# Gated recurrence: the first rows of the second recurrence (keys and queries times gates) on GpSimd instead of VectorE

## The reference, cut to what matters

```python
def step(carry, inp):
    S, R = carry
    q_t, k_t, v_t, a_t, aR_t, b_t, g_t = inp
    kn = k_t / jnp.maximum(jnp.linalg.norm(k_t, axis=-1, keepdims=True), 1e-12)
    pred = jnp.einsum('bhji,bhj->bhi', S, kn)
    r = jnp.clip(v_t - pred, -CLIP, CLIP)
    S = a_t[..., None] * S
    kp = jnp.einsum('bhd,bhde->bhe', kn, S)
    S = S + b_t[..., None, None] * kn[..., None] * (v_t - kp)[..., None, :]
    o = jnp.einsum('bhji,bhj->bhi', S, q_t)
    R = aR_t[..., None] * R
    kpR = jnp.einsum('bhd,bhde->bhe', kn, R)
    R = R + g_t[..., None, None] * kn[..., None] * (r - kpR)[..., None, :]
    o = o + jnp.einsum('bhji,bhj->bhi', R, q_t)
    return ((S, R), o)
```

## Time and profile before

| what | value |
|---|---|
| median of 3 runs | 3036.23 us (3035.22 to 3039.76) |
| span of the profiled execution | 3029.5 us |
| the rounds of the recurrence, from the first `begin` to the last fill | 919.6 to 1910.3 us of the span |
| busy in that stretch (990.7 us) | PE 774.1, DVE 861.8, ACT 444.2, POOL 381.8 us |
| granted TensorE clock in that stretch | 0.92 of full speed |

### The profile page before, as it was taken

One profiled execution on the slowest core, in us unless ns is written; L12 is line 12 of the kernel. 1 busy time (PEld: TensorE's weight loads), 2 busy tenths in 40 slices (PEclk: granted clock), 3 DMA queues, 4 the chain that ended last, 5 costly groups with the idle time before them and its releaser, 6 DMA issues. The chain is left out here.

```text
span 3029.5 us, 119908 instructions
## 1 busy us (share of the span) xinstructions
PE 2443.0 (81%) x51995; PEld 1879.4 (62%) x51995; DVE 2046.8 (68%) x4945; ACT 1381.3 (46%) x3266; POOL 958.9 (32%) x1170
## 2 busy tenths in 40 slices
PE   8978477999976787877888787659998997798754
PEld 6755465555555576767767676547876554576633
DVE  3448336777748988989888889257777666664752
ACT  5443233444443445544444443437776554463420
POOL 0000324665640633344333344211111441261004
PEclk9979778999988899999999998879999998897876
DMA  3200431111110000000000000002222003242014
GB/s 100 63 1 29 122 105 53 46 46 46 46 62 3 4 4 4 5 4 4 4 4 4 4 4 4 3 17 60 63 60 67 3 3 106 59 110 68 6 42 120
DMA packets 80349, 118.09 MB, mean 39 GB/s; under 512 B 11360, under 2 KB 66160, under 8 KB 79296
## 3 DMA queue, kind: packets, MB, share of 16 engines
q1 hardware_dynamic: 71312, 100.66, 10.7%
q0 software_dynamic: 8576, 10.53, 1.7%
HBM read 98.51 MB, written 16.51 MB: 38 GB/s over the span
## 5 line engine op out<-in xcount | busy, mean ns | idle before, releaser
L3174 PE MATMUL psum<-l1d_rw,l1d_cols 64*32 64x32 f32 (+2 forms) x20480 | 244.4, 216 | 107.7 <-issue 88.1
L3174 PEld LDWEIGHTS psum<-l1d_rw,l1d_cols 64*32 64x32 f32 x20480 | 211.8, 108 | 151.2 <-issue 126.9
L2469 POOL TENSOR_SCALAR l1xs_p<-l1xs_p,l1xs_col 128x257 f32<-128x257 f32 x256 | 233.8, 932 | 204.7 <-DVE l1xs_col L2425 204.7
L2894 POOL TENSOR_TENSOR l1d_tmp<-l1d_lt,l1d_xi 128x64 f32<-128x64 f32 (+1 forms) x96 | 41.7, 463 | 634.0 <-DVE l1d_xi L3525 632.7
L2390 ACT ACTIVATE l1xs_p<-psum,l1xs_col 128x257 f32<-128x257 f32 x256 | 120.0, 474 | 209.1 <-DVE l1xs_col L2420 203.1
L3432 DVE TENSOR_TENSOR l1d_rw<-l1d_rw,l1d_tots 128x1536 f32<-128x1536 f32 x96 | 151.9, 1582 | 45.7 <-PE psum L3174 45.2
L2432 DVE STREAM_TRANSPOSE l1xs_pt<-l1xs_p 128x288 f32<-128x288 f32 x256 | 122.4, 478 | 79.4 <-POOL l1xs_p L2469 79.4
L3111 PE MATMUL psum<-l1d_src,l1d_wp 128*128 128x128 f32 x1024 | 139.0, 293 | 3.2 <-issue 1.9
L2354 PE MATMUL psum<-l1xs_pt,l1xs_vals 32*128 32x512 f32 x1152 | 136.6, 604 | 0.0
L2342 PE MATMUL psum<-l1xs_keys,l1xs_qx 128*32 128x257 f32 x2048 | 130.9, 389 | 4.3 <-DVE l1xs_qx L2414 2.8
L3111 PEld LDWEIGHTS psum<-l1d_src,l1d_wp 128*128 128x128 f32 x1024 | 128.4, 204 | 7.4 <-issue 4.1
(11 more groups left out here) (558 smaller groups left out, 6845.5 us busy)
## 6 DMA issues: line engine op xcount, KB each, us to landing
l2f_w<-in_l2f_w SPq DMA_DIRECT2D x16, 768.0 KB
l1xs_vals<-in_ctx_strips SPq DMA_DIRECT2D x16, 576.0 KB
l0f_w<-in_l0f_w SPq DMA_DIRECT2D x15, 579.0 KB
l0x_ctxT<-in_ctxT SPq DMA_DIRECT2D x16, 516.0 KB, 3.7
l1xs_keys<-in_ctxT SPq DMA_DIRECT2D x16, 516.0 KB
l2x_ctxK<-in_ctxT SPq DMA_DIRECT2D x64, 129.0 KB, 2.1
l2x_ctxV<-in_ctxT SPq DMA_DIRECT2D x64, 129.0 KB, 2.1
l3f_w<-in_l3f_w SPq DMA_DIRECT2D x15, 193.5 KB
```

The lines of the kernel that those rows point to most:

```text
L2469: nc.gpsimd.tensor_scalar(p[:, t % 4, :S2], p[:, t % 4, :S2], col[:, 2, t % 4:t % 4 + 1], None, ALU.mult).then_inc(s["norm"], 1)
L3174: mm = nc.tensor.matmul(k.ps[bank0 + pr + e // per * 2][b * T:b * T + T, e % per * w:(e % per + 1) * w], cols[rr, 2 * n, e * 128 + b * T:e ...
```

## The change

`begin` for R leaves DVE. A new function `begin_r` on POOL does the same three multiplications. POOL runs it for round 0 ahead of its loop, and for round i + 1 ahead of the merges of round i. DVE gets a wait on `rowR` in level 0 of `advance`, since that step overwrites the keys' products that POOL read.

```diff
+            def begin_r(i):
+                odd = lambda x: x.rearrange("p g (n two) -> p g n two", two=2)[:, :, :, 1]
+                even = lambda x: x.rearrange("p g (n two) -> p g n two", two=2)[:, :, :, 0]
+                pool.wait_ge(s["kn"], i * 8 + 8)
+                pool.wait_ge(s["q"], i * 2 + 2)
+                pool.wait_ge(s["gate"], i * 4 + 4)
+                if i > 0:
+                    pool.wait_ge(s["mR_mm"], i * LEVELS)
+                tt(rw[:, 6], rw[:, 1], ar[:], ALU.mult)
+                tt(even(rw[:, 5]), odd(rw[:, 3]), even(ar[:]), ALU.mult)
+                tt(odd(rw[:, 5]), odd(rw[:, 4]), odd(ar[:]), ALU.mult).then_inc(s["rowR"], 1)
+
+            begin_r(0)
             for i in range(NT):
+                if i + 1 < NT:
+                    begin_r(i + 1)
                 pool.wait_ge(s["turn"], 2 * i + 2)
...
                 dve.wait_ge(s[mm], i * LEVELS + lv + 1)
+                if lv == 0:
+                    dve.wait_ge(s["rowR"], i * LEVELS + 1)
...
             begin(0, a, 0, 2, "rowS")
-            begin(0, ar, 6, 5, "rowR")
...
                     begin(i + 1, a, 0, 2, "rowS")
-                    begin(i + 1, ar, 6, 5, "rowR")
```

## The result

| | before | changed |
|---|---|---|
| median, us | 3035.72 (3034.02 to 3039.76, 4 runs) | 3100.09 (3097.84 to 3106.03, 4 runs) |
| ratio to before | | 1.0214, 95% interval 1.0197 to 1.0232 |
| span of the profiled execution, us | 3029.5 | 3104.2 |

The change costs 64 us, 2.1%. The forecast was 3084 (48 us), its range 3058 to 3106. The profiled execution of the changed kernel took 3106.03 us with a span of 3104.2, so 1.8 us lie around the span, not the 6.7 I assumed; the traced execution of the kernel before was some 4 us faster than its median, and the two spans lie 74.7 us apart.

The account below looks back on a forecast made before the run. No engine was full; the S rows and the fill before `keep_s` set the pace. Span 3029.5 plus 16 x 3.0 = 48 us gave 3078, plus 6.7 us outside the span 3084 us; range 3058 to 3106.

Parts of the forecast that it names:

- DVE isn't late at `keep_s`, so its relief is worth next to nothing: End of a round: DVE waits for the fill in 13 of 16 rounds, so the removal alone saves some 1.5 us.
- The wait in front of `keep_s`: DVE's wait for the S fill, expected to grow from 16.5 to about 33 us in total.
- POOL and DVE exclude each other, first come, in turn; masked copies are free of it: At `begin` for S, two-SBUF-input operations alternate: `rowS` at +7.55 instead of +3.25 us after the keys; `keep_r` untouched.
- POOL's lengths: POOL's R-row multiplications: keys 2.43 us, halves 1.30 each; upper ends 3.02 and 1.51, 1.0 us more a round.
- The fill starts 3 us later on average, 48 us: PE's fill follows the late S rows, putting `keep_s` at +9.6 against +6.6 us; 16 x 3.0 = 48 us.
- A fill takes 1.84 us: PE's S-row fill between `rowS` and `keep_s`, sized at its earlier mean, 29.5 / 16 = 1.84 us.
- The rival of the lower clock: PE's longer idling lowers its clock every round, 0.8 + 0.6 us more for fill and projection: 3106 us, chance 0.08.
- All of it is on the path: After the fill, PE's and DVE's following work shift together, so the whole 48 us reaches the total time.
- shared ports: At `begin` for S both engines run at about half speed: 16 us, 3052; chance 0.09 with a half-absorbed shift.
- without a hold: At `begin` for S POOL doesn't block DVE in these shapes, so nothing is lost: 3035 us, chance 0.06.
- the relief counts in full: DVE's removed multiplications in each round save their full 37 us: 2999 us, chance 0.02.

Follow-up runs that it names:

- the first experiment: The changed kernel with POOL waiting for the S rows (`rowS`) before its three multiplications: 3049.64 us, 1.0016 of the kernel before.
- the fourth experiment: The changed kernel with five POOL memsets in place of its multiplications, R rows left zero: 3043.18 us, 1.0014 of the kernel before.
- the second profile: The changed kernel run and profiled again without any edit: 3103.5 us, 1.0200 of the kernel before.
- the two with the swap: PE's S fill moved ahead of `values`: in the changed kernel with POOL also waiting for `rowS`, 1.0098; in the kernel before, 1.0092.
- the second experiment: The changed kernel with POOL making only the keys, DVE the two R halves behind `begin` for S: 3069.18 us, 1.0080 of the kernel before.
- the seventh experiment: The changed kernel with PE doing `step_out` before the fill: 3116.44 us, 1.0255 of the kernel before.

## Why the prediction was right, and what it missed

- *DVE isn't late at `keep_s`, so its relief is worth next to nothing.* Right. The first and the fourth experiment remove the three multiplications without the exclusion and stand within 0.4% of the kernel before; the wait took up what was removed. The wait in front of `keep_s`, which I put at 33 us in the change, is 49.2, because `keep_s` starts at +10.3 on average instead of +9.6.
- *POOL and DVE exclude each other, first come, in turn; masked copies are free of it.* Right: 2.69, 1.99 and 1.98 us against the expected 2.9, 2 and 2. The fourth experiment adds that POOL's memsets, which only write, don't do it.
- *POOL's lengths.* The keys at 2.43 by estimate are 2.38 without DVE. The halves I took at 1.30, the contiguous row's side; they are 1.52, the upper end. Between turns of DVE they took about 1.36 net, so this cost little: the S rows come at +7.34 instead of +7.55.
- *The fill starts 3 us later on average, 48 us.* Right: it starts 7.39 us after the keys instead of 4.47, 46.7 us in 16 rounds (PE's wait for the S rows grew by 47.4).
- *A fill takes 1.84 us.* This is the term that was mis-sized. It takes (35.6 + 10.2) / 16 = 2.86 from first to last, and 2.62 in the second profile, (31.5 + 10.5) / 16. I took the mean busy time of fills that mostly began well behind the S rows, and put it straight behind them. The rival of the lower clock named one part of it (+6.1 us, and +2.0 in the second profile; for fill and projection together I had priced 22); the stops inside the fill (+8.7, and +9.0) nobody had named, though the earlier trace rows has 1.5 us of them under "issue". With them `keep_s` is 60 us later in the sum of the rounds (56 in the second profile), where the sum had 48.
- *All of it is on the path.* Right: 61 and 58 us more between the keys and `keep_s` than in the first and the fourth experiment, 59 and 63 more in the span.
- The rivals with shared ports (3052) and without a hold (3035) are out by the lengths of `begin` for S. That the relief counts in full (2999) is out by the first experiment.

## What to carry to other kernels

Before work goes from VectorE to GpSimd, look at what VectorE executes in the same microseconds: an operation with two SBUF inputs beside a reading GpSimd operation waited for the whole of it, and here that held up the one result TensorE was about to need. The same work started 3.4 us later, behind that result, cost nothing that these runs can tell. And a stretch of matmuls that is moved up to the result which releases it need not be as long as before: look for stops of TensorE in it that the profile puts down to "issue", and count their end from the release and not from the stretch's own start.

## What the runs showed of the hardware that I had not expected

A fill stops at fixed places of TensorE's list of instructions, for up to 2.5 us, and how long it stops depends on how soon it starts behind the S rows. Most stops are in rounds 3, 5, 7, 9 and 11: in round 7 after 104 matmuls and in round 3 after 122 wherever a kernel with `values` ahead of the fill and `step_out` behind it stops there, after 109 and 127 in the two with the swap. Round 3 in the changed kernel:

```profile
1108.42 2.36 PE L3190 MATMUL psum<-l1d_rw,l1d_cols 64*32 64x80 f32 x122 [2.66 <-DVE l1d_rw L3431]
1112.38 0.49 PE L3190 MATMUL psum<-l1d_rw,l1d_cols 64*32 64x80 f32 x6 [1.60 <-issue]
```

The matmul behind such a stop starts 3.4 to 4.1 us after the S rows in 44 of the 45 stops that the sixteen fills have in the ten profiles, whether TensorE waited for the S rows or not. Two cases without a wait, round 5 of the kernel before and round 7 of the second experiment:

```profile
1217.32 1.49 PE L3174 MATMUL psum<-l1d_rw,l1d_cols 64*32 64x80 f32 x113
1219.34 0.38 PE L3174 MATMUL psum<-l1d_rw,l1d_cols 64*32 64x80 f32 x15 [0.53 <-issue]
```

```profile
1363.51 1.41 PE L3188 MATMUL psum<-l1d_rw,l1d_cols 64*32 64x80 f32 x104
1366.94 0.49 PE L3188 MATMUL psum<-l1d_rw,l1d_cols 64*32 64x80 f32 x24 [2.02 <-issue]
```

In the first the S rows were there at 1215.54, 1.78 us before the fill; it stopped for 0.53 us and went on 3.80 us after them. In the second they were there at 1363.17, 0.34 us before the fill; it stopped for 2.02 and went on 3.77 us after them. So work that TensorE still has when the S rows come uses up the stop. That is why the fills stop for 1.5 us in the kernel before, 10.2 in the change and 1.0 in the seventh experiment, where those five fills start 2 to 3.4 us after the S rows.

The trace also shows what came just ahead of the end of each stop: a packet in the DMA queue that brings instructions. That queue in the rounds of the changed kernel (packets, MB, share of the 16 engines' time):

```profile
q8 instruction: 237, 3.88, 1.5%
```

These are 237 packets of 16 KB for the 60,359 matmuls and weight loads of the same stretch, one for each 255. In round 7 a packet started at 1385.97 and took 1.26 us, and the fill went on at 1388.62, 1.4 us after its end. All 45 stops end 1.3 to 1.6 us after such a packet; about a tenth of all matmuls in the rounds start at that distance from one. The packet started 1.0 to 1.8 us after the S rows in 44 of the 45. So the stops go with the arrival of instructions. The Trainium skill (Runtime: NRT & Kernel Launch, section Instruction fetch mechanics) says that each engine's instructions are streamed in from memory in blocks of 256, at a cost that is mostly hidden. The trace agrees on the blocks, with one packet for each 255; in these fills the cost is not hidden, 10.2 us in the change. Why the packet comes only behind the S rows stays open: no run here moved it otherwise.
